# A masked depthwise convolution and its normalisation: the first image loaded over two queues by partitions

## The reference, cut to what matters

```
x: (4, 96, 128, 128) float32
pooled = x.mean(axis=(2, 3))                        # per image and channel
t  = relu(gamma * (pooled @ w1.T - mean) * rsqrt(var + 1e-5) + beta)     # 24 values
wt = (t @ w2.T + b2).reshape(b * 96, 1, 3, 3) * MASK  # per image and channel; 4 taps left:
                                                    # up-left, up, up-right, left
y  = depthwise_conv3x3(x, wt) + bias                # each image has its own weights
out = y * rsqrt(einsum("nchw,ic->nihw", y * y, gamma_eff) + beta_eff)
```

## Time and profile before

| | us |
|---|---|
| median of 3 runs | 259.08 (258.37 to 260.37) |
| the profiled execution | 260.12 |
| its span, first to last instruction | 258.2 |
| VectorE busy | 204.8 (79%) |
| TensorE busy | 199.3 (77%) |
| ScalarE busy | 186.3 (72%) |
| GpSimd busy | 169.7 (66%) |

### The profile page before, as it was taken

How to read it: one execution, slowest core, us unless ns; L and a number is a source line. 1 busy time by engine, 2 the same in 40 slices (tenths; PEclk the granted TensorE clock), 3 DMA queues, 4 the chain that set the end, 5 groups by cost and what they waited for, 6 DMA issues and landing times.

```text
span 258.2 us, 2123 instructions
## 1 busy us (share of the span) xinstructions
PE 199.3 (77%) x480; PEld 79.2 (31%) x480; DVE 204.8 (79%) x237; ACT 186.3 (72%) x203; POOL 169.7 (66%) x90
## 2 busy tenths in 40 slices
PE   0024221976999689999969899999698999999973
PEld 0021220322333333434324433333234333433220
DVE  6373239894599985999996699999959999999934
ACT  2220447693799568999974999999689866778472
POOL 2000000039597769899949699999499999999910
PEclk9999999995899959999995999999999999999967
DMA  7999999993429997987999989969835555566584
GB/s 204 243 245 240 243 241 240 244 243 121 143 82 223 309 284 258 300 242 227 262 323 285 274 280 290 271 213 255 307 109 164 176 164 162 150 187 187 148 254 131
DMA packets 13584, 57.63 MB, mean 223 GB/s; under 512 B 2595, under 2 KB 2598, under 8 KB 10886
## 3 DMA queue, kind: packets, MB, share of 16 engines
q1 hardware_dynamic: 13424, 57.22, 78.5%
q10 hardware_dynamic: 150, 0.29, 0.4%
HBM read 26.05 MB, written 25.17 MB: 198 GB/s over the span
## 4 chain that ended last, share of the span: by engine, by line
issue 38%; POOL 32%; DVE 13%; PE 8%; DMA 4%; ACT 2%; POOLq 0%; SPq 0%; ACTq 0%
POOL norm L585 26%; DVE acc L557 8%; POOL sq L574 6%; PE den L519 5%; DVE y L565 4%; DMA out_y<-norm 4%; ACT norm L427 1%; PE den L527 1%; PE acc L500 1%; ACT sq L405 1%; DVE y L567 0%; ACT norm L420 0%; DVE norm L733 0%; PE acc L501 0%; SPq L302 0%
## 5 line engine op out<-in xcount | busy, mean ns | idle before, releaser
L557 DVE SCALAR_TENSOR_TENSOR acc<-ximg,taps,acc 128x1016 f32<-128x1016 f32 x96 | 122.6, 1277 | 26.6 <-ACT acc L398 14.3
L585 POOL TENSOR_TENSOR norm<-y,norm 96x1024 f32<-96x1024 f32 x45 | 105.7, 2361 | 54.3 <-ACT norm L427 54.0
L519 PE MATMUL den<-sq,gam_e 96*96 96x512 f32 x252 | 124.7, 640 | 17.5 <-ACT norm L427 6.7
L427 ACT ACTIVATE norm<-den,beta_e 96x1024 f32<-96x1024 f32 x63 | 69.2, 1102 | 18.4 <-PE den L519 16.6
L519 PEld LDWEIGHTS den<-sq,gam_e 96*96 96x96 f32 x252 | 41.6, 174 | 91.1 <-issue 73.5
L500 PE MATMUL acc<-ximg,diag 128*128 128x512 f32 x108 | 58.3, 622 | 9.6 <-DVE y L567 9.6
L565 DVE SCALAR_TENSOR_TENSOR y<-ximg,taps,acc 128x1016 f32<-128x1016 f32 x48 | 61.1, 1273 | 1.7
L405 ACT ACTIVATE sq<-y 96x1024 f32<-96x1024 f32 x48 | 49.7, 1049 | 10.8 <-DVE y L567 10.7
L585 POOL TENSOR_TENSOR norm<-yd,norm 96x1024 f32<-96x1024 f32 x15 | 35.4, 2359 | 15.7 <-ACT norm L427 15.7
L368 ACT ACTIVATE pool_out<-ximg 128x1920 bf16 (+3 forms) x18 | 34.2, 1902 | 4.0 <-DMA ximg<-in_x 4.0
L574 POOL TENSOR_TENSOR sq<-yd 96x1024 f32<-96x1024 f32 x15 | 28.4, 1892 | 5.8 <-DMA yd<-y 5.8
(11 more groups left out here) (53 smaller groups left out, 46.5 us busy)
## 6 DMA issues: line engine op xcount, KB each, us to landing
out_y<-norm SPq DMA_DIRECT2D x63, 384.0 KB, 3.5
ximg<-in_x SPq DMA_DIRECT2D x12, 816.0 KB, 11.8
ximg<-in_x SPq DMA_DIRECT2D x8, 768.0 KB, 9.7
yd<-y SPq DMA_DIRECT2D x48, 128.0 KB, 3.7
ximg<-in_x SPq DMA_DIRECT2D x12, 272.0 KB, 12.6
ximg<-in_x SPq DMA_DIRECT2D x12, 256.0 KB, 9.7
ximg<-in_x SPq DMA_DIRECT2D x4, 720.0 KB, 6.9
out_y<-norm SPq DMA_DIRECT2D x2, 192.0 KB, 2.4
```

Source lines behind the costliest of these rows:

```text
L427: nc.scalar.activation(norm[:, g], den[0:C, g % 2], ACT.Abs_reciprocal_sqrt, bias=beta_e[:, 0:1]).then_inc(normed, 1)
L519: ins = nc.tensor.matmul(den[0:C, g % 2, j:j + BANK], gam_e[:, :], sq[:, g, j:j + BANK], start=True, stop=True)
L557: nc.vector.scalar_tensor_tensor(out=tap_to(sums(u, s), tap), in0=tap_in(b, u, s, tap), scalar=tap_w(b, s, tap), in1=tap_to(sums(u, s), ta ...
L585: nc.gpsimd.tensor_tensor(norm[:, g], quarter(u, g), norm[:, g], ALU.mult).then_inc(scaled, 1)
```

## The change

Each piece is now three DMAs: partitions 0 to 63, 64 to 95 and 96 to 127 (`load_rows`, `SPLIT = 64`), and its semaphore counts 48. Of image 0, SyncE issues the first of the three for pieces 0 to 5 in order; ScalarE issues the other two, in the order of pieces 1, 0, 3, 2, 5, 4, with the bias rows after its first piece. SyncE waits for all six pieces of image 0 before it issues image 1. Images 1, 2 and 3 are loaded by SyncE alone, three DMAs per piece.

```diff
--- before.py
+++ after.py
@@ -102,6 +102,8 @@
     G = P // TAPS
     BIAS_PARTS = 3
     CUT = QR // 2
+    SPLIT = 64
+    LOADS = 3 * 16
     PIECES = [(h, s) for h in range(2) for s in range(SLOTS)]
     ACT_SLOT, PE_SLOTS = 1, (0, 2)
     CONVS = UNITS * SLOTS
@@ -110,6 +112,8 @@
     TAPS_UNIT = UNITS - 2
 
     LAST_PIECE = len(PIECES) - 1
+
+    OTHER_ORDER = (1, 0, 3, 2, 5, 4)
     POOL_ON_ACT = ((0, "all"), (2, "all"), (4, "all"), (LAST_PIECE, "top"))
     POOL_ON_DVE = ((1, "all"), (3, "all"), (LAST_PIECE, "end"))
     ACT_POOLS = len(POOL_ON_ACT)
@@ -284,16 +288,22 @@
             return out[b, :, r:r + UR, :].rearrange("c r w -> c (r w)")
 
 
-        def load_piece(sp, b, i):
+        def load_rows(queue, b, i, p0, p1):
 
             h, s = PIECES[i]
             r0, r1 = piece_rows(h)
-            top = max(r0, 1) if s == 0 else r0
-            a = s * QR - 1
-            sp.dma_start(img(b)[0:C, s, top * W:r1 * W], flat[b, :, (a + top) * W:(a + r1) * W]).then_inc(x_loaded[i], 16)
-            a = SLOTS * QR - 1
-            sp.dma_start(img(b)[C:P, s, r0 * W:r1 * W],
-                         flat[b, s * CD:(s + 1) * CD, (a + r0) * W:(a + r1) * W]).then_inc(x_loaded[i], 16)
+            if p0 < C:
+                top = max(r0, 1) if s == 0 else r0
+                a, c0 = s * QR - 1, p0
+            else:
+                top, a, c0 = r0, SLOTS * QR - 1, s * CD + p0 - C
+            queue.dma_start(img(b)[p0:p1, s, top * W:r1 * W],
+                            flat[b, c0:c0 + p1 - p0, (a + top) * W:(a + r1) * W]).then_inc(x_loaded[i], 16)
+
+        def load_piece(sp, b, i):
+            load_rows(sp, b, i, 0, SPLIT)
+            load_rows(sp, b, i, SPLIT, C)
+            load_rows(sp, b, i, C, P)
 
         def move_d(sp, b, u, s):
 
@@ -318,7 +328,7 @@
             h, s = PIECES[i]
             sp.wait_ge(convolved, 2 * conv_no(b, 2 * h + 1, s) + 2)
 
-            sp.wait_ge(x_loaded[i], 32 * (b + 2))
+            sp.wait_ge(x_loaded[i], LOADS * (b + 2))
             load_piece(sp, b + 2, i)
 
         def sp_unit(sp, b, u):
@@ -344,7 +354,7 @@
         def first_pool(engine, i, part_of):
 
             r0, r1 = first_rows(i, part_of)
-            engine.wait_ge(x_loaded[i], 32)
+            engine.wait_ge(x_loaded[i], LOADS)
             src = img(0)[:, PIECES[i][1], r0 * W:r1 * W]
             col = len(PIECES) if part_of == "end" else i
             if engine is nc.vector:
@@ -361,7 +371,7 @@
             h, s = PIECES[i]
             r0, r1 = piece_rows(h)
             r0 = max(r0, 1)
-            act.wait_ge(x_loaded[i], 32 * (b + 1))
+            act.wait_ge(x_loaded[i], LOADS * (b + 1))
             src = img(b)[:, s, r0 * W:r1 * W]
             n = (b - 1) * len(PIECES) + ACT_POOLS + k
             act.wait_ge(pooled_act, n - 1)
@@ -600,9 +610,10 @@
         def _(sp):
             sp.wait_ge(pads_zeroed, 1)
             for i in range(len(PIECES)):
-                load_piece(sp, 0, i)
+                load_rows(sp, 0, i, 0, SPLIT)
             for i in range(len(PIECES)):
-                sp.wait_ge(x_loaded[i], 32)
+                sp.wait_ge(x_loaded[i], LOADS)
+            for i in range(len(PIECES)):
                 load_piece(sp, 1, i)
             for s in range(SLOTS):
                 move_d(sp, 0, 0, s)
@@ -616,9 +627,13 @@
         @block.scalar
         def _(act):
             act.dma_start(par_s[:, :], par[:, :]).then_inc(par_loaded, 16)
-            act.wait_ge(bias_zeroed, 1)
-            for i in range(BIAS_PARTS):
-                act.dma_start(bias_f[32 * i:32 * i + 1, 0], biasrow[:, :]).then_inc(bias_loaded, 16)
+            for k, i in enumerate(OTHER_ORDER):
+                load_rows(act, 0, i, SPLIT, C)
+                load_rows(act, 0, i, C, P)
+                if k == 0:
+                    act.wait_ge(bias_zeroed, 1)
+                    for j in range(BIAS_PARTS):
+                        act.dma_start(bias_f[32 * j:32 * j + 1, 0], biasrow[:, :]).then_inc(bias_loaded, 16)
             act.wait_ge(warm_set, 1)
             nc.scalar.activation(warm[:, :], warm[:, :], ACT.Abs_reciprocal_sqrt).then_inc(warmed, 1)
```

## The result

| | before | after |
|---|---|---|
| median, us (runs) | 258.80 (258.37 to 260.37, 4) | 267.75 (266.37 to 269.71, 4) |
| profiled execution | 260.12 | 269.71 |
| its span | 258.2 | 267.8 |
| mean granted TensorE clock of the core | 0.945 | 0.938 to 0.940 in all four |

The ratio is 1.034 (95% interval 1.026 to 1.042): 9 us slower where the forecast was 3.8.

What follows compares the result with a forecast made beforehand. DMA engines, full until about 58 us, were taken as the bound, so image 1's end moves the kernel's end nearly one for one. −0.8 + 2.2 + 1.4 + 1.0 = +3.8 us gave 263.0 us, range 256 to 268.

Steps and rivals of the forecast that it cites:

- rival C: All loads: the split is dear, every stretch at 213 to 218 GB/s; +11 us, 270 us; chance 0.1.
- Step 1: Image 0 through two queues: served in order of issue, mostly one half of the partitions at a time; −0.8 us.
- the prediction's own sign: ACT's bias rows at the start: landing near 17 us shows order of service, before 8 us a round robin.
- rival A: Image 0: the queues run side by side all the way, 322 to 366 GB/s; 254.5 to 257 us; chance 0.2.
- rival B: Image 0: queues overlap but often meet on the same half, 275 to 285 GB/s; 258 to 261.5 us; chance 0.2.
- Step 2: Between images 0 and 1: SyncE's wait for all of image 0 leaves a gap in DMA; +2.2 us.
- Step 3: Image 1 on one queue in three transfers per piece: 230 GB/s instead of 242; +1.4 us (0 to +2.9).
- Step 4: Images 2 and 3 in the same three transfers: more DMA time where little is left; +1.0 us (0 to +3).
- Step 5: First hidden layer: piece 4 lands last, ACT pools it late, taps +2.0 us, covered by GpSimd's 4.10 us wait.
- Step 6: Set-up on ACT: ten more issues put the table load at about 8.1 us, bias rows near 16 to 17; costs nothing.

Runs made afterwards that it cites:

- e9: Kernel before with block 0's three moves `yd<-y` issued on ScalarE's queue while SyncE's is full of image 1; 260.01 us, no ratio.
- e1: Kernel before with every piece of all four images loaded in three transfers (0-63, 64-95, 96-127) by SyncE alone, waits as before; 267.48 us, ratio 1.035.
- e17: Repeat of e2: kernel before with SyncE waiting for all six pieces of image 0 before it issues image 1; 264.51 us, ratio 1.021.
- e8: Kernel before with three transfers per piece (0-63, 64-95, 96-127) for images 2 and 3 only; 261.83 us, ratio 1.006.
- e10: e1 with the three transfers cut at partitions 32-95, 0-31 and 96-127, still one queue; 256.63 us, no ratio.
- e3: Changed kernel with images 1 to 3 loaded in two transfers per piece (96 and 32 rows) as before; 263.10 us, ratio 1.017.
- e5: Kernel before with each piece as one DMA over all 128 partitions, source rows 64 KiB apart, other values computed; 245.22 us, one run.
- e2: Kernel before with SyncE waiting for all six pieces of image 0 before it issues image 1; 264.78 us, ratio 1.015.
- e12: e10 with each store of 96 partitions also cut in two, 32-95 and 0-31; 252.39 us (249.12 to 262.34).
- e15: e12 once more, unchanged, in twelve runs; 257.38 us (249.33 to 264.67).

## Why the prediction was wrong

The direction was right, the size more than twice the forecast's; 267.75 lies just inside the range, which was wide enough to hold the lower part of rival C. In the profiled executions the 9.6 us are +1.0 (image 0), +2.2 (gap), +3.2 (image 1) and +3.2 (behind the square), where the forecast had −0.8, +2.2, +1.4 and +1.0. By its own steps:

**Step 1, image 0 (−0.8, measured +1.0): failed, in mechanism and size.** "Transfers are fed in the order of issue over both queues" is refuted twice: both queues carry 46 to 56% of the engines' time from 12 to 20 us, and e9's moves overtake image 1. The bias rows, the prediction's own sign, decide nothing: they are there when VectorE asks at 12.35, not near 16, but the 16 took SyncE's six issues to be over by 3.9 us, and they last until 4.86 (3.78 us from 1.08), so fewer of them stood ahead. So the queues were side by side, which was rival A's condition, and A was wrong too: sharing brought 247 and 238 GB/s, not 322 or more. What happened is rival B's sharing at no more than the rate of before. The Trainium skill, DMA: Bandwidth & Descriptors, Rules for kernel authors, calls two transfers to disjoint partition halves not worth the bother; for image 0 the measurement agrees as far as the kernel before goes (+1.0 us), while against the same three-way cut on one queue (e1, +2.7) the second queue was worth 1.7 us. The high 366 and 322 of the earlier trace rows say nothing on two queues either: of the 0.37 MB of the first, 0.24 are image rows of SyncE's queue, and most of the second is the start of that queue alone. No packet of ScalarE's queue moves from 3.3 to 4.5 us in the kernel before, and the rate is

```profile
3.30:4.50 1.20, 0.00 (x0) 0.00 (x0) 0.73 (x4) 0.70 (x1) 0.00 (x0) 1.00 1.15 301
```

From 4.5 to 6 us it is down to 234. What makes the start so fast stays open.

**Step 2, the gap (+2.2): right.** No byte moves from 30.5 to 32.5 us, and e17 is shifted by 1.3 to 2.9 us from the square until 185 us.

**Step 3, image 1 (+1.4): mis-sized, +3.2.** I took 230 GB/s, since handovers between the halves would help. The rows show 216 to 222, which is +2.4 to +3.2 for 6.44 MB; the 3.2 is the 6.4 of shift at the square, less 1.0 and 2.2. e1 shows the cut's rate (224 to 227) without a second queue. 218, the end that I kept for the range (+2.9), was the value: the nearest row was that of a transfer on one half, and there was no row for a handover.

**Step 4, images 2 and 3 (+1.0): not shown.** e8's ratio (+1.5, 0.2 to 2.8) holds it, but its trace has no such shift. The sign that the prediction named did come, DMA waits of 4.3 + 3.9 + 3.5 = 11.7 us between 75 and 200 us over the present 7.5, and e8 with the same transfers has 7.2. What is measured behind the square is +3.2, and it cannot be told apart from the clock: 0.92 against 0.94 is up to 3.6 us, the delay grows in the half-clock stretches, and all four runs after have 0.938 to 0.940 where before has 0.945 to 0.972 in the experiments' runs that the ratios rest on. **This term was missing in the prediction**: where TensorE falls to half clock is not fixed, it differs between the traces, and each such stretch costs up to half its length. Why it falls there stays open.

**Step 5, the pooling tail: right and covered.** ScalarE pools piece 4 from 31.42 and the taps come 3.0 later (1.0 + 2.0); GpSimd waits 6.83 us for moves.

**Step 6, the set-up: right,** table load at 8.46 (8.1 forecast); the bias rows came earlier than it said, which cost nothing.

**Rival C** (+11, every stretch at 213 to 218) had a tenth of the chance and came nearest: the profiled executions differ by 9.6. It was right on image 1 (+2.9) and wrong on image 0 (+3.0, measured +1.0), so its sum is near in part by luck: it had no clock in it. At the square the parts nearly add up (+4.2 for the cut alone, +1.7 for the gap alone, +6.4 for both with the second queue). The medians do not, since the cut alone is 3.5% slower, the gap alone 2.1%, and the whole change 3.4%; what lies between, the clock's share in each, was not separated.

What holds a cut at 225 and another at 260? The Trainium skill, SBUF — State Buffer, Door 1, gives the partitions below 64 the even ports and the others the odd ones. Transfers of 0 to 63, 64 to 95 and 96 to 127 then write one half each, and 32 to 95 both; e1 and e10 agree in which is the faster (225 and 261). The ports by themselves do not explain e3 and the kernel after: there both halves are written at a time by two queues, which would leave room for up to 435 (an estimate, the prediction's), and 247 were measured, 66 ns per KB of a packet (0.563 x 16 x 8 us over 1.09 MB) against 38 in e5 and 72 in e1. What two queues meet on was not tried apart. Shown is that the cut of the destination sets the rate; why, is argued.

## What to carry to other kernels

A load of all 128 partitions in one transfer (425 GB/s) is worth more than a second queue (247): where the layout forbids it, try the cut first (one edit, 225 against 261 GB/s), and a cut whose large transfer has partitions of both halves. A wait that empties the queue costs its 2 us in full where the queue sets the pace. A difference of a few us between two traces should be held against the granted clock by stretch before it is explained by data.

## What the runs showed of the hardware

- 128 rows in one transfer: 425 GB/s, at 64 KiB between source rows and at none. 96 and 32 rows: 238 to 244 in the kernel before, up to 249 in e8. 64, 32 and 32 rows from partition 0: 224 to 227. The same with the 64 rows in the middle (e10): 256 to 263.
- Two queues on disjoint halves share the 16 engines evenly, and together move no more than the 96 and 32 rows of one queue (247 and 238 against 238 and 243), but more than the same three transfers on one (227 and 225, e1).
- A transfer on an idle queue, while the other one is full, took 8.5 us for 128 KB where 2.2 is undisturbed; the first of them began to move 5.8 us after its issue.
- TensorE's granted clock falls to half at different places and for different times in different traces: 16.46 of 16.90 us busy in the one of e2, and mean clocks of 0.928 and 0.967 over e2's kernel, with 271.37 and 260.39 us.
- One kernel can load at two rates: e12 and e15, the same text, had 281 and 257 GB/s in 12 to 20 us. Why is open.
